# Fusion transformer block on one core: moving a norm, a coefficient step and three sets of copies between engines

## The reference

```python
h = concatenate([patches(x) @ W.T + b, txt], axis=1)            # 8 x 548 x 192
# attention on the normed h, three heads of 64
q, k, v = xn @ Wq.T, xn @ Wk.T, xn @ Wv.T                       # xn = layernorm(h)
scores  = (q @ k.T) / 8 * decay            # decay = gamma ** (m - l), 0 where m < l
o = softmax(scores) @ v
o = (o - mean) / sqrt(var + eps)           # group norm per sample and head
h = h + (o * gn_weight + gn_bias) @ Wo.T
# mixture of 16 experts on the normed h, the eight best by the router
comb = top-8 weights of softmax(xn2 @ router.T), normalised     # xn2 = layernorm(h)
h = h + sum_e comb[:, e] * (gelu(xn2 @ w1[e]) @ w2[e])
```

## Time and profile before

| what | value |
|---|---|
| median of 3 runs | 759.21 us |
| profiled execution | 758.52 us, its span 756.7 us |
| PE busy | 717.0 us, 95% |
| VectorE busy | 575.1 us, 76% |
| ScalarE busy | 468.8 us, 62% |
| GpSimd busy | 159.5 us, 21% |

### The profile page before, as it was taken

How to read it: one execution, slowest core, us unless ns; L and a number is a source line. 1 busy time by engine, 2 the same in 40 slices (tenths; PEclk the granted TensorE clock), 3 DMA queues, 4 the chain that set the end, 5 groups by cost and what they waited for, 6 DMA issues and landing times.

```text
span 756.7 us, 13058 instructions
## 1 busy us (share of the span) xinstructions
PE 717.0 (95%) x4205; PEld 599.2 (79%) x4205; DVE 575.1 (76%) x1591; ACT 468.8 (62%) x1049; POOL 159.5 (21%) x278
## 2 busy tenths in 40 slices
PE   6988999999998978999999999999999999999995
PEld 5777889888887757887887887887887887888895
DVE  7898888988887846777777677777777777776774
ACT  3678788778787726455555555555555555555553
POOL 3062574574542980000000000000100100000000
PEclk9999999999999998999999999999999999999998
DMA  6700011012112641552462462663562562552441
GB/s 197 212 23 21 3 44 44 3 44 59 51 44 67 202 127 29 114 124 73 105 168 71 104 171 67 129 147 67 135 142 66 138 137 68 132 131 52 94 87 40
DMA packets 124357, 70.57 MB, mean 93 GB/s; under 512 B 85792, under 2 KB 104288, under 8 KB 124288
## 3 DMA queue, kind: packets, MB, share of 16 engines
q1 hardware_dynamic: 124288, 69.74, 37.1%
HBM read 58.65 MB, written 10.63 MB: 92 GB/s over the span
## 4 chain that ended last, share of the span: by engine, by line
PE 72%; ACT 9%; DVE 7%; POOL 4%; issue 3%; POOLq 2%; SPq 1%; DVEq 1%; DMA 0%; ACTq 0%
PE ps L1446 71%; ACT pt L695 3%; ACT ot L695 2%; ACT pr L775 1%; DVE pr L1128 1%; PE ps L1595 1%; POOL w_lo L651 1%; ACT k_hi L695 1%; DVE sc L1106 1%; POOL xn L574 1%; DVE xb L1069 1%; POOLq L650 1%; ACT xa_hi L695 1%; DVE xa_lo L1069 1%; POOL w_r L649 1%
## 5 line engine op out<-in xcount | busy, mean ns | idle before, releaser
L915 ACT ACTIVATE act<-ps 128x512 f32<-128x512 f32 (+1 forms) x216 | 124.5, 577 | 189.1 <-PE ps L1446 188.5
L1337 DVE TENSOR_TENSOR act<-act,gate 128x512 f32<-128x512 f32 (+1 forms) x216 | 145.4, 673 | 109.3 <-ACT act L915 88.8
L1446 PE MATMUL ps<-x,w_hi 128*128 128x512 f32 (+1 forms) x648 | 215.3, 388 | 6.8 <-ACT act L915 6.8
L1446 PE MATMUL ps<-x,w_lo 128*128 128x512 f32 (+1 forms) x432 | 165.7, 384 | 0.0
L1446 PEld LDWEIGHTS ps<-x,w_hi 128*128 128x128 f32 x648 | 120.9, 189 | 33.5 <-ACT act L915 8.3
L1069 DVE TENSOR_TENSOR act_lo<-act,act_hi 128x512 fp32r<-128x512 f32 (+1 forms) x216 | 144.2, 668 | 0.2
L695 ACT ACTIVATE act_hi<-act 128x512 fp32r<-128x512 f32 (+1 forms) x216 | 130.3, 603 | 6.7 <-DVE act L1337 6.5
L1446 PEld LDWEIGHTS ps<-x,w_lo 128*128 128x128 f32 x432 | 81.4, 189 | 16.7
L546 POOL TENSOR_TENSOR rstdb<-vepsb,neg_half 128x4 f32<-128x4 f32 x9 | 9.6, 1071 | 367.9 <-DVE vepsb L1192 367.9
L1446 PE MATMUL ps<-act_hi,w_hi 128*128 128x512 f32 (+1 forms) x216 | 83.6, 387 | 2.2 <-DVE act_lo L1069 2.0
L1446 PE MATMUL ps<-act_hi,w_lo 128*128 128x512 f32 (+1 forms) x216 | 83.2, 385 | 0.0
(11 more groups left out here) (187 smaller groups left out, 1196.5 us busy)
## 6 DMA issues: line engine op xcount, KB each, us to landing
gate<-comb_dram SPq DMA_DIRECT2D x128, 256.0 KB, 4.2
w_raw<-w SPq DMA_DIRECT2D x16, 384.0 KB, 3.7
h_dram<-h SPq DMA_DIRECT2D x8, 384.0 KB
res<-h_dram SPq DMA_DIRECT2D x8, 384.0 KB, 4.1
rb<-h_dram SPq DMA_DIRECT2D x48, 64.0 KB, 2.6
out<-rb SPq DMA_DIRECT2D x48, 64.0 KB, 1.9
x_dram<-xn_t SPq DMA_DIRECT2D x24, 96.0 KB, 2.4
gate<-comb_dram SPq DMA_DIRECT2D x16, 144.0 KB, 3.1
```

Source lines behind the costliest of these rows:

```text
L915: a.activation(act[j % 3][:, 0:n], ps[:, up_bank(j), 0:n], ACT.Gelu_apprx_tanh).then_inc(gelu_done, 1)
L1337: dve.tensor_tensor(act[j % 3][:, 0:n], act[j % 3][:, 0:n], gate[e % 4][:, 0:n], ALU.mult).then_inc(gated, 1)
L1446: return pe.matmul(dst, w, x, start=start, stop=stop)
```

## The change

Four things move.

1. The scaling of the second feed-forward tile leaves GpSimd (`norm_second` goes) for ScalarE, in two pairs of instructions behind steps 5 and 7 of the first tile. GpSimd keeps the doubling copy. The semaphore counts of later tiles move by one accordingly.
2. On GpSimd the last batch's group-norm coefficients stand in front of the splits of parts 4 to 7 of w2, and no longer between parts 6 and 7.
3. In the attention loop ScalarE makes the first two groups of the third head's copies before it rounds the second k, and the first chunk of x before the o copies. PE no longer waits for VectorE before the first group's transposes.
4. The copy of `k2_hi` to the lower half leaves ScalarE for VectorE.

```diff
-            split_w2(2)
-            second_rstd(1)
-            pool.drain()
-            pool.wait_ge(x2t_done, 2)
-            norm_second()
-            for p in range(3, W2_PARTS - 1):
+            second_rstd(1)
+            split_w2(2)
+            split_w2(3)
+            second_twice(1)
+            gn_coefficients(LB)
+            for p in range(4, W2_PARTS):
                 split_w2(p)
-            gn_coefficients(LB)
-            split_w2(W2_PARTS - 1)
...
                 qk_round(b, 2)
+                if tail:
+                    pt_copy(t, 2, (0, 1))
                 qk_round(b, 3)
                 if tail:
-                    pt_copy(t, 2)
-                a.wait_ge(qk_hi, nth(b, 5, 4))
-                copy(k2_hi[0:HD, :], k2_hi[HD:P, :]).then_inc(qk_hi, 1)
+                    pt_copy(t, 2, (2, 3))
...
                     pt_copy(b, 1)
+                    x_hi(b + 1, 0)
                     o_copy(b, 0, O_BANKS[0])
-                    x_hi(b + 1, 0)
                     x_hi(b + 1, 1)
...
+                elif k == 5:
+                    second_norm(1, 0)
+                elif k == 7:
+                    second_norm(1, 1)
...
                     sub(two(lo), src, two(hi)).then_inc(qk_lo, 1)
+                dve.tensor_copy(k2_hi[0:HD, :], k2_hi[HD:P, :]).then_inc(qk_hi, 1)
...
-            dve.wait_ge(ln2_normed, t)
+            dve.wait_ge(ln2_normed, t + 1)
...
+                    probs_transpose(t, 2, (0,))
                     pe.wait_ge(qk_lo, nth(b, 4, 1))
-                    probs_transpose(t, 2, (0, 1, 2))
+                    probs_transpose(t, 2, (1, 2))
```

More of the change, by code:

```diff
@@ L427, in load_res @@
             def load_res(t):
[L429 to L432, removed]
+                if t >= 3:
+                    sp.wait_ge(ln2_normed, t - 2)
                 r = width(t) // segs(t)
@@ L566, in norm_next @@
                 pool.tensor_copy(xn[:, :, D:256], xn[:, :, P:D]).then_inc(xn_ready, 1)
[L568 to L574, removed]
-                pool.drain()
-                pool.tensor_copy(xn2[:, :, D:256], xn2[:, :, P:D]).then_inc(xn2_ready, 1)
             def halve_w1(b):
@@ L639, in second_twice @@
             def second_twice(t):
-                twice(ln2_normed, 1, xn2, xn2_ready)
+                twice(ln2_normed, t + 1, xn2, xn2_ready)
             def split_w2(p):
@@ L1180, in second_part @@
                     dve.wait_ge(ld_res[t % 3], 16 * (t // 3 + 1))
[L1181 to L1184, removed]
+                    if t >= 2:
+                        dve.wait_ge(ln2_normed, t)
                 for g in ((0, 1), range(2, n), ())[part]:
```

## The result

| | us |
|---|---|
| before, 4 runs on the same chip | 760.17 (758.96 to 761.2) |
| changed, 4 runs | 767.12 (766.56 to 769.61) |
| ratio, 95% interval | 1.0106 [1.0088, 1.0123] |
| profiled execution, its span | 766.7, 764.9 |

The kernel is 1.06% slower. The direction was foreseen; the size was not: +4.1 us had been worked out, and +7.0 came by these two medians. The ratio implies a kernel before of 759.1 us (767.12 / 1.0106), and against that the loss is 8.0 us, close to the 8.2 us by which the two profiled spans differ. The median of 767.12 lies just inside the range that had been given (758 to 767.5), at its upper end.

What follows compares the result with a forecast made beforehand. TensorE, 95% busy, was taken as the bound, with VectorE becoming it in the attention batches. Loss 11.2 less gain 7.1 gave +4.1 us; the median was predicted at 762.8 us, range 758 to 767.5.

Steps and rivals of the forecast that it cites:

- Two loops of almost one length: Attention batches: the PE and ScalarE chain repeats every 27.29 us, and VectorE waits only 0.40 us.
- The walk: Attention batches: VectorE's loop followed between first decays; VectorE free at 28.3 + c, losing 1.0 us + c per batch.
- c: Attention batches: price of the 64x548 SBUF-to-SBUF copy on VectorE, taken as 0.44 + 0.58 = 1.02 us, ends 0.44 and 1.54.
- the copy waits for GpSimd's whole subtraction: Rival, attention batches: c = 1.54, loss 13.9, net +6.8, time 766 us; chance 0.17.
- The clock stays full, I think, as these waits are about 2 us.: Attention batches: PE's waits in the third head's scores, about 2 us, were to leave its clock full.
- in front of batch 7 ... VectorE is not late there: 0: Last interval between batches: without the layer statistics of 1.37 us VectorE is not late, loss 0.
- The feed-forward gain: Feed-forward stage: 5.92 us wait gone and 1.47 us of clock back, less 0.3 us: 7.1 us gained.
- the cover of the norm: Feed-forward stage: second norm pair ends near 267.5, over 6 us before PE's transposes, so the norm costs nothing.
- what is late next: Feed-forward stage: product whose gated values follow a gelu ending only 0.7 us early; 0.3 us off, 0 to 1 possible.
- Nothing is lost there: Feed-forward stage: w2 parts after the coefficients come in time, first near 274.3, needed after 285; no loss.

Runs made afterwards that it cites:

- the first experiment: Changed kernel with the attention loop put back as in the kernel before, so only the feed-forward part stays: 753.08 us, ratio 0.9922.
- the weight copies alone: On the first experiment's kernel, the third head's first two copy groups ahead of the second k's rounding, PE's first transposes unheld: 755.43 us, ratio 0.9955.
- the copy from PSUM: Changed kernel with VectorE making the lower half of k_hi straight from PSUM, ahead of its subtraction: 763.55 us, ratio 1.0059.
- the halved subtraction: Changed kernel with GpSimd's 548-column subtraction for y written as two instructions of 274 columns: 763.66 us, ratio 1.0062.
- the parts held: On the first experiment's kernel, GpSimd holds the splits of w2's parts 6 and 7 until down(11)'s operand is made: 753.26 us, ratio 0.9921.

## Why the prediction was right in direction and wrong in size

- **What bounds the kernel**: right. Two loops of almost one length, with VectorE the next bound; the copy and the reorders turned it into the bound, and PE's waits for `mx` are the 10.0 us shown.
- **The walk**: right within 0.5 us where both reorders stand without the copy, 28.3 us against 27.77 to 28.24. Over batches 1 to 6 the reorders were put at 5 x 1.0 - 0.25 = 4.75 us and cost 4.1 (140.16 where the first experiment has 136.06). For the weight copies alone the walk was 0.5 us per period too high (28.0 against a mean of 27.5).
- **The failed step: c, the price of the copy.** The prediction took 1.02 us, "the wait that a row shows: c = 0.44 + 0.58". Measured: the copy takes 0.92 us in batch 2, then 1.36 to 1.52, and delays what stands behind it on VectorE by 0.85, 1.30, 1.45, 1.28 and 1.28 us in batches 2 to 6 (from the start of `k_lo` to the first decay, against the run with the copy on ScalarE). Over batches 1 to 6 the copy was to add 5 x 1.02 = 5.1 us. These delays sum to 6.2, and the five intervals grew by 7.2 (147.35 less 140.16); the last 1.0 lies in the intervals with the slow clock, next point. 0.58 us had been borrowed from another pair of instructions. It is the rest of GpSimd's instruction in that meeting and says nothing of this one. The prediction had the right numbers beside it: the copy due at 26.0, GpSimd's subtraction 0.3 us ahead of it and running until 27.1. In the trace it was 0.30 us ahead. Given a hold for the whole instruction, which 0.74 against 0.16 us already suggested, the price follows from these two times alone: 1.1 plus the copy, 1.54; the trace has 1.1 plus 0.30. This is the mechanism of the rival "the copy waits for GpSimd's whole subtraction", to which 0.17 had been given. That its time of 766 comes so near 767.12, and its loss of 13.9 us between the batches so near the 13.8 measured, is in part luck: it has 7.7 us for c where 6.2 were measured, and neither the 1.4 us of batch 7 nor the slow clock.
- **A term put at nothing: the clock.** "The clock stays full, I think, as these waits are about 2 us." It did not: three of the five intervals between batches 1 and 6 have a granted clock of 0.94. Those three exceed the delay of the copy by 0.33, 0.48 and 0.37 us, and the two at 1.00 do not exceed it; in all about 1.0 us. This share is read from the stretches; no run changed the clock alone. Where the copy from PSUM or the halved subtraction made the waits for `mx` shorter (1.1 and 1.45 us at most), the clock stayed at 1.00 in every interval, though no limit can be read from this, since a wait of 1.42 us came before one of the changed kernel's three falls; with x's order undone it fell again after waits of 1.70 and 1.77 us, and there each slow interval is about 1.2 us longer than its neighbours.
- **Its companion: "in front of batch 7 ... VectorE is not late there: 0".** The interval grew by 1.42 us (28.73 against 27.31). By the prediction's own numbers VectorE would have been free at 28.3 + c - 1.37, which is 27.95 with c = 1.02 and 28.3 with the measured copy, and not by 27.3. The line was written without adding c. VectorE has no idle time ahead of that decay in the trace:

```profile
232.84 1.38 DVE L1087 CAST k_hi<-k_hi 64x548 fp32r<-64x548 f32 x1
234.25 0.79 DVE L1125 BATCH_NORM_STATS2 gst<-ot 128x6 f32<-128x274 f32 x2
235.06 0.73 DVE L1097 CUSTOM_DVE_ANT_0 sc<-ps,decay 128x548 f32<-128x548 f32 x1
```

- **The rule behind it.** The Trainium skill (SBUF — State Buffer, section "SBUF: two separate sides") says that of a VectorE instruction that needs the shared pair and a GpSimd instruction the one that starts first has it for its whole length, and the other fully blocks. The runs agree: 1.36 us behind a whole instruction, 0.82 behind half of one, 0.73 from PSUM also inside GpSimd's instruction.
- **The feed-forward gain**: 7.1 predicted, 6.1 measured. The 5.92 us wait and the slow clock went, as foreseen, and the cover of the norm held. The term that failed is the 0.3 us for "what is late next": the wait of down(11) went from 0.77 to 1.90 us, as VectorE's gate and subtractions met GpSimd's splits of w2. I had written of the parts after the coefficients "Nothing is lost there", since I asked only whether they come in time, and not beside what they run. With them held back, 503.06 and 502.86 us remain of 510.39, a gain of 7.3 to 7.5.
- **Not in the sum**: 0.85 us more ahead of the first decay. At this place the change adds nothing that would account for it; the profiled executions of all kernels spread there from 25.64 to 27.92 us. In the trace PE starts on the patches, which a DMA brings, at 12.57 us where it did at 11.36 before.

Of the 4.1 us between the sum and the spans, c makes 1.1, the clock 1.0, batch 7's interval 1.4, the feed-forward gain 1.0 and the start 0.85, so no single term carries the miss, though the two that come of c make 2.5; the reorders, batch 0 to 1 and the stretch behind batch 7 give back 0.65, 0.3 and 0.3.

## What to carry to other kernels

When an SBUF-to-SBUF operation moves to VectorE, or a GpSimd instruction moves in time, write down for both engines when each instruction with SBUF on both sides starts and ends: the price of a meeting is the rest of the other's instruction, and here 0.7 us decided between 0.15 us and 0.9 to 1.1. A wait that this puts on TensorE can cost a second time, through its clock: look at the granted clock of each stretch before putting it at nothing. Ask of each thing that is moved earlier not only who waits for it but what it will now run beside. And where a reorder makes an engine idle with work queued behind, look for an independent instruction to fill the idle time before giving the reorder up: here it turned a loss of 0.9 us into a gain of 2.3.

## What the hardware showed beyond that

- The copy of 64x548 from SBUF to SBUF takes 0.43 us and the same from PSUM 0.73; the slower one, in an earlier place, was the better one beside GpSimd.
- Not only copies are held: a VectorE operation with both tensors in SBUF went from 0.68 to 1.38 us (`act<-act,gate`) and from 0.73 to 1.46 (`y<-ot,y`) beside GpSimd's splits, while one with an operand in PSUM (`k_lo<-ps,k_hi`) stayed at 0.72 to 0.73 in all 16 instances of the changed kernel. GpSimd's cast, with one input, holds as well (0.58 us in place of 0.43). And the hold goes both ways: GpSimd's `w_r<-w_raw,w_r` at 298.15 takes 1.07 us beside the `y` subtraction of VectorE, and 0.60 where none runs.
- Executions differ in two places that no edit touched. From batch 7's first decay to up(2) nine profiled executions take 25.6 to 25.9 us and the other five 26.7 to 27.0 (first experiment 25.85, with the parts held 27.00): in the nine the granted clock of that stretch is 1.00, in the five it is 0.94. The first decay moves by up to 2.3 us at a clock of 1.00; with it moves the time at which PE starts on the patches that a DMA brings (11.36 to 12.71 us), and the twelve matmuls on them then take 4.24 to 5.41 us. Why was not tested.
- The time of an execution goes with its mean granted clock. With the copy back on ScalarE, the five executions at 0.992 took 759.36 to 760.42 us and the five at 0.997 or 0.998 took 757.61 to 758.69. That hides effects near 1 us in the medians, and a comparison stretch by stretch was needed to see them.
